# One irregular order of attention's products for a whole pair of heads, and ten double row maxima a pair instead of four

## The reference

```
Q, K, V = xn @ Wq + bq, xn @ Wk + bk, xn @ Wv + bv        # 16 heads of 16 numbers
scores  = einsum('bqhd,bkhd->bhqk', Q, K) * 16 ** -0.5 + alibi[h, q, k]
attn    = softmax(scores, axis=-1)                        # over 1024 keys
out     = einsum('bhqk,bkhd->bqhd', attn, V) @ Wo + bo
```

## Time and profile before

| what | value |
|---|---|
| median of 3 runs | 2366.53 us (2364.92 to 2369.34) |
| span of the profiled execution | 2364.1 us |
| median of the runs less that span (what lies around the instructions) | 2.4 us |
| granted TensorE clock, mean | 0.998 |
| PE, DVE, ACT, POOL busy | 99%, 84%, 72%, 43% of the span |

### The profile page before, as it was taken

The page is one execution under the profiler, slowest core; times in us unless marked ns, Lnnn a source line. Parts: engine busy times, 40 slices in busy tenths (PEclk is TensorE's granted clock), DMA queues, the critical chain, the costliest instruction groups (busy, mean ns, idle before and its releaser), DMA issues.

```text
span 2364.1 us, 51756 instructions
## 1 busy us (share of the span) xinstructions
PE 2329.9 (99%) x19966; PEld 1561.3 (66%) x19966; DVE 1985.7 (84%) x3243; ACT 1712.9 (72%) x3279; POOL 1012.0 (43%) x1013
## 2 busy tenths in 40 slices
PE   7999999999999999999999999999999999999998
PEld 6874444444444444444444448999999989988998
DVE  7889999999999999999999956777777765555555
ACT  4447889888999999999999987777777763333332
POOL 2112556553225555454454324343433354455444
PEclk9999999999999999999999999999999999999999
DMA  8984545543224444343443325777777753344432
GB/s 304 379 323 171 168 157 163 160 147 95 83 86 133 121 128 131 111 127 120 117 127 113 106 92 177 234 244 238 238 245 234 245 179 107 108 124 128 123 107 90
DMA packets 189750, 383.15 MB, mean 162 GB/s; under 512 B 54164, under 2 KB 100756, under 8 KB 176292
## 3 DMA queue, kind: packets, MB, share of 16 engines
q1 hardware_dynamic: 151536, 219.17, 28.9%
q0 software_dynamic: 36880, 159.87, 21.1%
q10 hardware_dynamic: 1088, 0.79, 0.1%
HBM read 247.86 MB, written 140.31 MB: 164 GB/s over the span
## 4 chain that ended last, share of the span: by engine, by line
PE 87%; DVE 8%; DMA 2%; issue 1%; ACT 1%; SPq 1%; POOL 0%; DVEq 0%; POOLq 0%; ACTq 0%
PE ps L534 84%; DVE mx L1010 5%; PE ps L547 3%; DVE mx L1013 2%; DMA Md<-mT 1%; SPq L1516 0%; ACT qkH L829 0%; DMA OPS<-Md 0%; DMA xr<-Xn 0%; ACT pta L849 0%; DMA xt<-in_x 0%; DVE qkL L1000 0%; ACT accs L856 0%; POOL rstd L1224 0%; DVE xn L984 0%
## 5 line engine op out<-in xcount | busy, mean ns | idle before, releaser
L1010 DVE TENSOR_REDUCE mx<-ps 128x1 f32<-128x512 f32 x1552 | 959.5, 676 | 4.9 <-PE ps L534 4.5
L534 PE MATMUL ps<-OPS 52*128 52x512 f32 (+1 forms) x4096 | 749.3, 446 | 4.8 <-DMA OPS<-Md 1.9
L534 PEld LDWEIGHTS ps<-OPS 54*128 54x128 f32 (+1 forms) x4096 | 359.0, 184 | 463.5 <-ACT pta L849 209.9
L849 ACT ACTIVATE pta<-ps 128x512 f32<-128x512 f32 x1024 | 541.1, 598 | 79.6 <-PE ps L534 71.9
L849 ACT ACTIVATE ptb<-ps 128x512 f32<-128x512 f32 x1024 | 536.3, 600 | 45.5 <-PE ps L534 37.6
L534 PE MATMUL ps<-OPS,WB 128*128 128x256 f32 (+2 forms) x2364 | 384.4, 315 | 3.1 <-DVE VB L1135 1.6
L534 PEld LDWEIGHTS ps<-OPS,WB 128*128 128x128 f32 (+1 forms) x2364 | 332.3, 182 | 28.2 <-issue 3.9
L534 PE MATMUL ps<-pta,VB 128*32 128x352 f32 (+1 forms) x4096 | 300.6, 388 | 0.1
L1013 DVE TENSOR_REDUCE mx<-ps 128x2 f32<-128x1024 f32 x248 | 300.2, 1210 | 0.2 <-PE ps L534 0.2
L534 PE MATMUL ps<-ptb,VB 128*32 128x352 f32 (+1 forms) x4096 | 300.2, 388 | 0.0
L1268 POOL TENSOR_SCALAR m<-m 128x16 f32<-128x16 f32 x64 | 16.9, 265 | 558.8 <-DVE m L1023 558.8
(11 more groups left out here) (171 smaller groups left out, 2865.8 us busy)
## 6 DMA issues: line engine op xcount, KB each, us to landing
OPS<-QKh SPq DMA_DIRECT2D x512, 64.0 KB
Xs<-zero POOLq DMA_DIRECT2D x71, 256.0 KB, 3.6
xr<-Xs SPq DMA_DIRECT2D x71, 256.0 KB, 5.3
Ys<-VB SPq DMA_DIRECT2D x71, 256.0 KB, 5.0
QKh<-qkH SPq DMA_DIRECT2D x16, 1024.0 KB, 7.3
QKl<-qkL SPq DMA_DIRECT2D x16, 1024.0 KB, 8.9
OPS<-QKl SPq DMA_DIRECT2D x256, 64.0 KB
asum<-Sd SPq DMA_DIRECT2D x64, 256.0 KB
```

The costliest lines, as they stand in the source:

```text
L534: return self.e.matmul(o, l, r, start=start, stop=stop)
L849: self.e.activation(pt(m)[:, half * GT:(half + 1) * GT], ps[:, n % 3, :], ACT.Exp).then_inc(sem["exp"], 1)
L1010: self.e.reduce_max(mx[:, r % 2, hh, i, half:half + 1], ps[:, bank, :], AX.X).then_inc(sem["mxred"], 1)
```

## The change

Three things change. The order of the products is now written out for a whole pair (four strings of PAIR, one for each two chunks), with S, u and P in irregular runs. The values are no longer cut by two chunks but are one stream of 8 x 512 columns a pair, cut at 13 places by WIDTHS; `values(lo, hi)` takes a stretch of that stream and splits it at chunk borders. And DOUBLE holds ten couples instead of four. The letter T marks `max_rows`, which stood in the code before. The first pair keeps the old order (FIRST_PAIR), so that values lie two chunks behind the scores as before.

```diff
-CUTS = (0, 352, 672, 2 * 512)
-ORDER = "SuSuSuPSuSuSuPSuSuP"
-FIRST_STEP = "SuSuSuLSuSuLSuSuLSu"
-DOUBLE = (2, 6, 10, 14)
+FIRST_PAIR = "SuSuSuLSuSuLSuSuLSu", "SuSuSuPSuSuSuPSuSuTP", "SuSuSuPSuSuSuPSuSuP", "SuSuSuPSuSuSuPSuSuP"
+PAIR = (
+    "SuSuPSuSuPuSuSSuPuS",
+    "SuuSPSuSuPSuSuPSuSuTP",
+    "SuuSPSuSuSuPuSuSuSPu",
+    "SuSPSuSuuSPSuuSuSP",
+)
+FIRST_WIDTHS = 352, 320, 352
+WIDTHS = 288, 192, 544, 352, 128, 384, 96, 320, 544, 192, 320, 544, 192
+STREAM = 8 * 512
+DOUBLE = (0, 1, 2, 3, 5, 7, 9, 11, 12, 14)
...
+def value_parts():
+
+    at = 0
+    for r in range(NPAIR + 1):
+        for width in FIRST_WIDTHS * 3 if r == 0 else WIDTHS if r < NPAIR else FIRST_WIDTHS:
+            yield at, at + width
+            at += width
...
-            for c in FIRST_STEP if s == 0 else ORDER:
+            for c in "PPP" if r == NPAIR else (PAIR if r else FIRST_PAIR)[kc // 2]:
...
-                    if s >= 2:
-                        self.values(*divmod(s - 2, 8), v)
-                    v += 1
+                    self.values(*next(self.parts))
...
-                for c in range(kc, kc + 2):
-                    at = slice(max(CUTS[v] - GT * (c - kc), 0), min(CUTS[v + 1] - GT * (c - kc), GT))
+                for x in range(lo // GT, (hi + GT - 1) // GT):
+                    at = slice(max(lo - GT * x, 0), min(hi - GT * x, GT))
+                    r, c = divmod(x, 8)
...
-                if kc == 6 and v == 2:
+                if hi % STREAM == 0:
```

More of the change, by code:

```diff
@@ L79, in wait_ge @@
             self.e.wait_ge(self.sem[name], value)
+def value_parts():
[4 more added lines that the diff above has]
+            at += width
 class Order:
     def run(self):
+        self.parts = value_parts()
         self.begin()
@@ L221, in attention @@
         if s % 2 == 0:
-            i = v = last = 0
-            for c in FIRST_STEP if s == 0 else ORDER:
+            i = last = 0
+            for c in "PPP" if r == NPAIR else (PAIR if r else FIRST_PAIR)[kc // 2]:
                 if c == "L":
@@ L227, in attention @@
                 elif c == "S":
-                    if r < NPAIR:
-                        self.scores(r, kc + i // 4, i // 2 % 2, i % 2)
+                    self.scores(r, kc + i // 4, i // 2 % 2, i % 2)
                     i += 1
@@ L234, in attention @@
                         n += 1
-                else:
-                    if v == 2 and kc == 2 and r + 1 < NPAIR:
-                        self.max_rows(r + 1)
-                    if s >= 2:
-                        self.values(*divmod(s - 2, 8), v)
-                    v += 1
+                elif c == "T":
+                    if r + 1 < NPAIR:
+                        self.max_rows(r + 1)
+                else:
+                    self.values(*next(self.parts))
             if s == 0:
@@ L305, in scores, with values @@
     def scores(self, r, kc, hh, half): pass
-    def values(self, r, kc, v): pass
+    def values(self, lo, hi): pass
     def heads(self, r, i): pass
@@ L637, in scores, with values @@
                         QO[h0:h0 + KEXP, k, half * GT:(half + 1) * GT], True, True).then_inc(sem["smm"], 1)
-            def values(self, r, kc, v):
-                b, j = divmod(r, NH // 2)
-                for c in range(kc, kc + 2):
-                    at = slice(max(CUTS[v] - GT * (c - kc), 0), min(CUTS[v + 1] - GT * (c - kc), GT))
-                    if at.start >= at.stop:
-                        continue
+            def values(self, lo, hi):
+                for x in range(lo // GT, (hi + GT - 1) // GT):
+                    at = slice(max(lo - GT * x, 0), min(hi - GT * x, GT))
+                    r, c = divmod(x, 8)
+                    b, j = divmod(r, NH // 2)
                     n = 16 * r + 2 * c
@@ L657, in values @@
                                            vb[:, b % 2, c, 32 * (2 * j + hh):32 * (2 * j + hh) + 32],
-                                           pt(n + hh)[:, half * GT:(half + 1) * GT][:, at], c == 0 and v == 0,
-                                           c == 7 and v == 2)
+                                           pt(n + hh)[:, half * GT:(half + 1) * GT][:, at],
+                                           c == 0 and at.start == 0, c == 7 and at.stop == GT)
                     if at.stop == GT:
@@ L849, in scores, with values @@
                 self.e.activation(pt(m)[:, half * GT:(half + 1) * GT], ps[:, n % 3, :], ACT.Exp).then_inc(sem["exp"], 1)
-            def values(self, r, kc, v):
-                if kc == 6 and v == 2:
+            def values(self, lo, hi):
+                if hi % STREAM == 0:
+                    r = hi // STREAM - 1
                     projections_over(self.w)
```

## The result

| | before | after |
|---|---|---|
| median of the runs | 2365.90 us (4) | 2388.35 us (4) |
| span of the profiled execution | 2364.1 | 2385.7 |
| score 0 of pair 0 to score 0 of pair 26 | 511.0 | 511.4 |
| to score 0 of pair 58 | 609.9 | 630.6 |
| to the last copy to `accs` | 118.8 | 119.4 |

What follows compares the result with a forecast made beforehand. DVE was taken to set 19.06 us a pair, PE to bound it at 19.01 afterwards. Steady pairs 2 plus router's pairs 3 gave 5 us: span 2364.1 to 2359, median 2361.5 against 2366.5; range 2345 to 2379.

Steps and rivals of the forecast that it cites:

- The rest at nothing: Terms priced at zero: ACT's exponentials, the copy to `accs`, the maxima's DMA, and DMAs keeping their places in SP's and POOL's queues.
- The third rival: Rival, 22%: short pieces and a thirteenth switch make PE slower than DVE was; 2375 us, or 2389 at the full price.
- PE's sum: PE's time for a steady attention pair: 18.62 for groups, switches and columns, plus 0.05, 0.27 and 0.07, together 19.01 us.
- The switches: PE's changes between score groups and value segments: 13 a pair instead of 12, each 0.143 us; the thirteenth segment costs 0.38.
- Short pieces: PE's value pieces of 32 to 96 columns, made by splitting at chunk borders: 0.05 us a pair.
- The upper bound: Highest price of PE's short value pieces, if no pass could be shorter than 0.108 us: 0.65 us a pair.
- The steady gain of 2 us: Gain over the 41 steady attention pairs, each going from 19.06 to 19.01 us: 2 us.
- the walk: Following one pair with trace latencies to find PE's remaining waits: 0.27 for scores, 0.07 for units; latencies good to 0.05.
- The router's pairs, 3 us: Between 195 and 572 us, twelve of 19 pairs carry router work on DVE; bound by DVE, gaining about 0.25 each: 3 us.
- DVE's floor: DVE's time a pair with six more double reductions and a fold wait: 19.06 - 0.38 + 0.1 = 18.78 us.
- the order doesn't matter: Rival, 12%: the loop of scores and exponentials costs 18.9 a pair by itself in either order; within 2 us, 2365.
- What would show it: Signs: 19.0 fold to fold, DVE idle 0.1 to 0.4 a pair, doubles 1.13 apart; against: slow short pieces, a shared-part gain.

## Why the prediction was wrong

**The step that failed** is "The rest at nothing", in its sentence "No DMA changes its place in SP's or POOL's queue." That is true of the order in the queue and says nothing of the time. The fold paces POOL, POOL paces the two indirect DMAs, and these moved by 0.4 to 0.5 us against PE's scores. Priced at nothing, the late news that came with this cost 19.8 us, 0.86 for each of 23 pairs, nearly all of the 20.7 us between the two stretches. The trace before showed that POOL waits for DVE's fold (361.0 us in 41 waits from 572 to 1353 us), and the DMAs stood in it; I read only the order and never asked what a transfer would newly coincide with. No rival covered it. The third rival had the right sign and the wrong cause. That this step failed is shown; why the DMAs at their new place hold back PE's news, and why not in every measurement, stays open.

**DVE.** Right: doubles 1.13 to 1.14 apart, but for the fourth, which starts 0.2 later (idle time behind couple 2, where it was forecast), the fold 0.71 behind its single (0.7 forecast), 0.15 idle a pair (0.1 to 0.4).

**PE's sum.** Right to 0.06: 19.07 a pair against 19.01. Thirteen switches of 0.14 to 0.16 and three score waits of 0.08 to 0.11 were there. The switches were put at 0.143, and 0.01 more on most of them is about what is missing.

**Short pieces.** I took 0.05, the pieces cost 0.01 each. The upper bound is refuted by the row of 620.09. The Trainium skill says that a product has some 60 cycles of overhead (TensorEngine Tiling (Array Packing), Instruction Overhead). By the forecast's estimate from that page, each of the four strips paying it in turn would have shown as 0.15 a piece; the trace does not agree with that reading. Whether four strips share it no run here shows, since the forecast counts 64 cycles for a pass of 32 columns.

**The steady gain of 2 us.** Not there: 19.07 against 19.06. The forecast gain was smaller than the error of the walk.

**The router's pairs, 3 us.** Failed. DVE's floor fell, but pairs 1 to 19 took 373.6 us together against 374.0 before, and pair 0 took 0.7 more; and the row of 195 to 572 us shows PE and DVE idle for 5.0 and 6.8 us, where both idled 3.4. My reading, which no run isolates: a pair there is neither DVE's nor PE's alone; the 0.6 that DVE does more holds up units at its place, and PE can't make up for it elsewhere, since it has its own waits. With both gains gone and the stalls absent, the kernel is about where the rival "the order doesn't matter" put it: 2368.9 to 2370.8 us, 0.04 to 0.18% above the kernel before. The number is luck, for the order does matter (57 us when it stands alone), and the rival's mechanism, a loop of scores and exponentials as long in the new order as in the old, is not what the trace shows. In the last three quarters of pair 62, which have no units, the changed kernel takes 14.03 against 14.26 before; with units (pair 24) it takes 14.45 against 14.35. So that loop alone got 0.2 shorter, and units and reductions take 0.4 a pair from the new order.

**What would show it.** I named what would be seen on DVE and PE and in the shared part, and nothing on ACT's waits for PE, where the loss stood plainest (1.4 against 0.4).

## What to carry to other kernels

When a change shifts one engine's phase against another's, list which DMAs hang on the shifted engine and where they land; queue order is not enough, and a test that delays them by 0.2 us costs little. Measure the slow kernel again beside each such test: where the loss doesn't come back on the same chip, a kernel without it proves nothing about the delay. If one engine's wait for another grows in its longest value and new rows appear with a common small count, look at one such event with all engines in order of time before thinking about the average pace. Double reductions and bursts of units only work together: compare the whole, then the halves.

## What the runs showed of the hardware

- What PE tells other engines can come 0.3 to 1.6 us late when POOL issues the second of two indirect DMAs, 1.33 to 1.37 apart, near a group of scores. PE waits for neither DMA and goes on: ACT and DVE are released in the same moment (907.69 and 907.72). The four updates of that group are recorded 0.034 us apart at 907.636 to 907.738, and that of the value product behind it, which ends by 907.03, follows at 907.831. This was seen in the first measurement and on one chip of five, at places that were free of it on other chips. Whether plain DMAs or a lone indirect one at the bad place do the same is not shown. Whether it is the write to PSUM or the news of it that is late, the trace can't say. By the Trainium skill's Perfetto Trace Analysis (Per-instruction lifecycle), TensorE's update follows PSUM's acknowledgement of the write, and the profiler's end of a product is an estimate; that agrees with rows in which PE looks on time and its readers are late.
- The Trainium skill's Trainium Architecture — The Big Picture (What this means for kernel authors) calls the engines independent processors, one of which doesn't block another unless a semaphore is put between them. Here PE, ACT and DVE wait for no semaphore of POOL's DMAs, and the late news that comes with these still cost 19.8 us of 2388: the rule doesn't cover this.
- A value product of 32 columns in four strips costs 0.01 us beyond its columns (32 + 288 columns in 0.69, 160 + 160 in 0.68).
